# Attention probabilities transposed by DMA instead of by TensorE, and scaled after the sum over keys

## What is computed

```python
x = x + xattn(layernorm(x), ctx)   # ctx: (128, 257, 96); 16 heads of 64
x = x + wkv(layernorm(x))          # time mixing with scans over the 32 tokens
x = x + moe(layernorm(x))          # 8 experts, argmax routing

def xattn(x, ctx):                 # for every sequence b
    q, k, v = x @ Wq, ctx @ Wk, ctx @ Wv      # split in 16 heads
    attn = softmax(q @ k.T / 8)               # (16 heads, 32 tokens, 257 keys)
    return (attn @ v, heads joined) @ Wo + bo
```

## Time and profile before

| what | value |
|---|---|
| median of 3 runs | 1026.83 us |
| the profiled execution, its own time | 1028.92 us |
| span of the profiled execution | 1027.0 us, 29818 instructions |
| busy in the span: PE / DVE / ACT / POOL | 85% / 81% / 67% / 75% |
| DMA packets' time, hardware queue | 15.9% of 16 engines |
| mean granted TensorE clock | 0.935 |

### The profile page before, as it was taken

One profiled execution on the slowest core, in us unless ns is written; L12 is line 12 of the kernel. 1 busy time (PEld: TensorE's weight loads), 2 busy tenths in 40 slices (PEclk: granted clock), 3 DMA queues, 4 the chain that ended last, 5 costly groups with the idle time before them and its releaser, 6 DMA issues.

```text
span 1027.0 us, 29818 instructions
## 1 busy us (share of the span) xinstructions
PE 870.6 (85%) x8554; PEld 720.6 (70%) x8554; DVE 831.1 (81%) x2343; ACT 684.0 (67%) x2029; POOL 774.3 (75%) x1237
## 2 busy tenths in 40 slices
PE   7989998999999999999999999999998461049895
PEld 7777786878787887878787887887776261036664
DVE  5899888989999989899999999998988657025563
ACT  3777776778777778778777777777775113037774
POOL 5788888898989898888889898989886503735554
PEclk9999999999999999999999999999999655559998
DMA  9111111111111111111111211111100840111120
GB/s 233 33 33 33 32 33 33 33 33 36 49 42 32 31 31 31 31 31 31 31 31 32 59 33 31 31 31 31 31 2 2 129 162 14 52 43 53 47 54 17
DMA packets 56836, 45.11 MB, mean 44 GB/s; under 512 B 8367, under 2 KB 54578, under 8 KB 56769
## 3 DMA queue, kind: packets, MB, share of 16 engines
q1 hardware_dynamic: 54464, 40.01, 15.9%
q0 software_dynamic: 2304, 4.25, 1.3%
HBM read 37.25 MB, written 7.52 MB: 44 GB/s over the span
## 4 chain that ended last, share of the span: by engine, by line
PE 36%; POOL 31%; issue 13%; DVE 12%; ACT 4%; DMA 1%; POOLq 1%; DVEq 1%; ACTq 0%; SPq 0%
POOL Pn L925 10%; PE bank L396 6%; PE bank L373 6%; PE bank L420 4%; POOL cT L916 4%; PE bank L1369 3%; PE bank L413 3%; PE bank L385 3%; POOL sorted_rows L1232 3%; POOL chi L906 2%; PE bank L1384 2%; DVE cs L839 2%; DVE nmax L783 2%; POOL clo L910 2%; DVE Tl L777 1%
## 5 line engine op out<-in xcount | busy, mean ns | idle before, releaser
L925 POOL TENSOR_TENSOR Pn<-Pe,rsum 128x1028 f32<-128x1028 f32 x128 | 243.1, 1899 | 74.4 <-DVE rsum L798 74.4
L713 ACT ACTIVATE Pe<-bank,nmax 128x257 f32<-128x257 f32 x512 | 240.5, 475 | 30.1 <-DVE nmax L783 29.5
L783 DVE TENSOR_REDUCE nmax<-bank 128x1 f32<-128x257 f32 x512 | 202.0, 415 | 35.3 <-PE bank L373 34.0
L373 PE MATMUL bank<-cT,qh 96*128 96x257 f16 x1024 | 184.8, 275 | 21.1 <-ACT Pe L713 19.6
L777 DVE TENSOR_TENSOR Tl<-bank,Th 128x512 f16<-128x512 f32 x256 | 173.8, 680 | 0.5 <-ACT Th L702 0.4
L702 ACT ACTIVATE Th<-bank 128x512 f16<-128x512 f32 x256 | 141.3, 595 | 48.5 <-PE bank L420 48.5
L420 PE MATMUL bank<-identf,Pn 128*128 128x128 f32 x1024 | 149.3, 274 | 0.0
L373 PE MATMUL bank<-cT,ql 96*128 96x257 f16 x512 | 139.2, 272 | 0.0
L420 PEld LDWEIGHTS bank<-identf,Pn 128*128 128x128 f32 x1024 | 115.1, 142 | 6.1
L373 PEld LDWEIGHTS bank<-cT,qh 96*128 96x128 f16 x1024 | 90.3, 97 | 38.3 <-issue 15.9
L713 ACT ACTIVATION_READ_ACCUMULATOR Pe<-bank,nmax 128x1 f32 x512 | 103.8, 203 | 0.0
(11 more groups left out here) (213 smaller groups left out, 2444.4 us busy)
## 6 DMA issues: line engine op xcount, KB each, us to landing
rawT<-in_dram SPq DMA_DIRECT2D x32, 385.5 KB, 3.9
raw<-in_dram SPq DMA_DIRECT2D x32, 384.0 KB, 4.4
sorted_rows<-fill SPq DMA_DIRECT2D x1, 2620.0 KB, 21.1
xs<-sorted_rows SPq DMA_DIRECT2D x40, 65.5 KB, 1.8
R<-in_dram SPq DMA_DIRECT2D x4, 512.0 KB, 5.9
Z<-last_rows SPq DMA_DIRECT2D x128, 2.2 KB
w1r<-in_dram SPq DMA_DIRECT2D x4, 512.0 KB, 13.7
w2fr<-in_dram SPq DMA_DIRECT2D x4, 512.0 KB, 14.2
```

Of the source, the lines that this page charges most:

```text
L373: last = nc.tensor.matmul(bank[SB[t]][:, 0:M], w[:, par, b, t * P:(t + 1) * P], cT[:, s4, c, 0:M], start=(k == 0), stop=(k == 2))
L713: nc.scalar.activation(Pe[:, n_par(j + 1), t, :], bank[SB[t]][:, 0:M], ACT.Exp, bias=nmax[:, n_par(j + 1), t:t + 1], accum_out=sums[:, n_p ...
L783: nc.vector.tensor_reduce(nmax[:, n_par(j + 1), t:t + 1], bank[SB[t]][:, 0:M], AX.X, ALU.max, negate=True).then_inc(s_nmax, 1)
L925: nc.gpsimd.tensor_tensor(Pn[:, par, :, :], Pe[:, par, :, :], rsum[:, par, :].unsqueeze(2).broadcast_to([P, QT, M]), ALU.mult)\
```

## The change

Scores now lie in four neighbouring banks (`quad`), two groups for each maximum. exp is not normalised and keeps no sums. Groups 2 and 3 go to Pe in SBUF, groups 0 and 1 stay in PSUM, in place. ScalarE rounds each pair to the f16 hi half; the lo half is made by VectorE (groups 0, 1) and GpSimd (groups 2, 3). Hi and lo lie in PHL, 2560 f16 columns, and one crossbar DMA on SP transposes all of it to PT (20 blocks of 128x128). `pe_pv` has the transposed probabilities as stationary operand and 97 context columns moving, 28 matmuls; the 97th column is 1, so it gives the row sum. VectorE takes the reciprocal of that column and scales the output into On. ScalarE and GpSimd split On into Ohl, and a second crossbar DMA (8 blocks) transposes it to OT, from which `pe_y` takes every fourth column. The sum over 16 heads is now kept in PSUM over four steps and added to x once. SP runs the pipeline too. Z is loaded once. chi moves from GpSimd to ScalarE. `pe_y` and the mixing come one step later.

The core of the diff, with lines left out at "...":

```diff
+        ORDER = (2, 3, 0, 1)
...
-        def pe_scores(n, par, b, s4, tiles):
+        def pe_scores(n, par, b, s4):
...
+            for k, t in enumerate(ORDER):
+                if t >= 2:
+                    wait(nc.tensor, s_exp, QT * (n - 1) + k + 1)
+                elif t == 0:
+                    wait(nc.tensor, s_Pl, n)
...
+        def pe_pv(n, par, s8, turns):
+            wait(nc.tensor, s_PT[par], 16 * turns)
...
+            wait(nc.tensor, s_On, n)
             for t in range(QT):
+                for k, (hl, w) in enumerate(((0, chi), (0, clo), (1, chi))):
+                    for c in range(MC):
+                        nc.tensor.matmul(O5[:, t, :], PT[:, par, (2 * t + hl) * MC + c, :], w[:, s8, c, 0:CW],
+                                         start=(k == 0 and c == 0), stop=False)
+                z = Z[:, bass.ds(n, 1), 0:CW].rearrange("p o c -> p (o c)")
+                last = nc.tensor.matmul(O5[:, t, :], PT[0:R3, par, QT * 2 * MC + t, :], z, start=False, stop=True)
             last.then_inc(s_PV, 1)
...
+                    o = OT[0:CC, gp, hl * QT + h // QT, :, :].rearrange("p b r -> p (b r)")[:, h % QT:GB * P:QT]
+                    last = nc.tensor.matmul(bank[7][:, 0:C], o, w[:, h, :],
+                                            start=(h == 0 and k == 0), stop=(h == H - 1 and k == 2))
...
         def pe_step(it, j):
             n, g, jj, gp = where(it, j)
             if exists(n + 1):
...
+                pe_scores(n + 1, ((j + 1) // GB) % NP2, (j + 1) % GB, (j + 1) % 4)
+            if exists(n - 1):
+                pe_pv(n - 1, (j - 1) % NP2, (j - 1) % NC8, 4 * it + (j - 1) // 2 + 1)
             if exists(n + 5):
-                pe_mix_free(it, j)
                 pe_q(n + 5, (j + 1) % GB, bass.ds(P * (g + 1 + (jj + 1) // GB), P))
...
-            if exists(n):
-                pe_probsT(n, n_par(j), 1)
...
         def act_step(it, j):
             n, g, jj, gp = where(it, j)
+            if exists(n + 4):
...
+                act_chi(n + 4, (j + 4) % NC8, par, (j + 4) % GB)
...
+                act_cT(n + 4, (j + 4) % 4, par, (j + 4) % GB)
+            if exists(n + 1):
+                p = n_par(j + 1)
+                for k, t in enumerate(ORDER):
+                    if k == 0:
+                        wait(nc.scalar, s_Pm, n)
+                    if k % 2 == 0:
+                        wait(nc.scalar, s_nmax, 2 * (n + 1) + k // 2 + 1)
+                    dst = Pe[:, p, t - 2, :] if t >= 2 else bank[t][:, 0:MP]
+                    nc.scalar.activation(dst, bank[t][:, 0:MP], ACT.Exp, bias=nmax[:, p, t:t + 1]).then_inc(s_exp, 1)
+                    if k == 1:
+                        wait(nc.scalar, s_PT[p], 16 * (4 * it + (j + 1) // 2))
+                    if k % 2:
+                        src = Pe[:, p, :, 0:MK] if t >= 2 else quad[:, 0:2, 0:MK]
+                        wait(nc.scalar, s_exp, QT * (n + 1) + k + 1)
+                        nc.scalar.activation(Pmain[:, p, t - 1:t + 1, 0, :], src, ACT.Copy).then_inc(s_Ph, 1)
+            if exists(n + 5):
+                act_q(n + 5, (gp + 1 + (jj + 1) // GB) % NP2, (j + 1) % GB)
             if exists(n - 1):
...
+                wait(nc.scalar, s_On, n)
+                nc.scalar.activation(Ohl[:, p, 0, :, 0:CC], On[:, p, :, :], ACT.Copy).then_inc(s_Oh, 1)
+            act_mix(*mixed(it, j))
...
         def dve_step(it, j):
             n, g, jj, gp = where(it, j)
+            if exists(n + 1):
+                dve_max(n + 1, n_par(j + 1), 0)
+            dve_stat_waits(it, j, g, jj)
+            if exists(n + 1):
+                dve_max(n + 1, n_par(j + 1), 1)
             dve_stat(it, j, g, jj, gp)
+            dve_mix_a(*mixed(it, j))
...
+            if exists(n - 1):
...
+                wait(nc.vector, s_PV, n)
+                nc.vector.reciprocal(rsum[:, p, :], O5[:, :, CC]).then_inc(s_rec, 1)
+                wait(nc.vector, s_rec, n)
+                nc.vector.tensor_tensor(On[:, p, :, :], O5[:, :, 0:CC], rsum[:, p, :].unsqueeze(2).broadcast_to([P, QT, CC]),
+                                        ALU.mult).then_inc(s_On, 1)
+            if exists(n + 1):
+                p = n_par(j + 1)
+                wait(nc.vector, s_Ph, 2 * (n + 1) + 2)
+                nc.vector.tensor_copy(Plast[:, p, 0:2, 0:2], quad[:, 0:2, MK:MP]).then_inc(s_hl, 1)
+                nc.vector.tensor_tensor(Pmain[:, p, 0:2, 1, :], quad[:, 0:2, 0:MK], Pmain[:, p, 0:2, 0, :], ALU.subtract)
+                wait(nc.vector, s_hl, n + 2)
+                nc.vector.tensor_tensor(Plast[:, p, 0:2, 2:3], quad[:, 0:2, MK:M], Plast[:, p, 0:2, 0:1],
+                                        ALU.subtract).then_inc(s_Pl, 1)
+            dve_mix_b(*mixed(it, j))
             if exists(n + 5):
                 dve_q(n + 5, (gp + 1 + (jj + 1) // GB) % NP2, (j + 1) % GB)
...
         def pool_step(it, j):
+            if exists(n + 4):
+                pool_clo(n + 4, (j + 4) % NC8, ((j + 4) // GB) % NP2, (j + 4) % GB)
+                pool_cT(n + 4, (j + 4) % 4, ((j + 4) // GB) % NP2, (j + 4) % GB)
             if exists(n + 1):
...
+                wait(nc.gpsimd, s_Ph, 2 * (n + 1) + 1)
+                nc.gpsimd.tensor_tensor(Pmain[:, p, 2:4, 1, :], Pe[:, p, :, 0:MK], Pmain[:, p, 2:4, 0, :], ALU.subtract)
+                nc.gpsimd.tensor_copy(Plast[:, p, 2:4, 0:2], Pe[:, p, :, MK:MP]).then_inc(s_hm, 1)
...
+            if exists(n - 1):
+                p = n_par(j - 1)
+                wait(nc.gpsimd, s_Oh, n)
+                nc.gpsimd.tensor_tensor(Ohl[:, p, 1, :, 0:CC], On[:, p, :, :], Ohl[:, p, 0, :, 0:CC], ALU.subtract)\
+                    .then_inc(s_Ol, 1)
...
+            def sp_step(it, j):
...
+                if exists(n):
+                    p = n_par(j)
+                    wait(sp, s_PV, n - 1)
...
+                    wait(sp, s_Pl, n + 1)
+                    sp.sem_inc(s_go)
+                    wait(sp, s_Pm, n + 1)
...
+                    sp.dma_start(PT[:, p, :, :], PHL[:, p, :], transpose=True).then_inc(s_PT[p], 16)
+                if jj == 0 and exists(g + 2, G) and (n_static(n) is None or g >= 0):
+                    load_ctx(g + 2, gp)
+                if exists(n - 2):
+                    wait(sp, s_y, GB * (2 * it + (j - 2) // GB) - GB)
...
+                    wait(sp, s_Ol, n - 1)
+                    sp.sem_inc(s_go)
+                    sp.dma_start(OT[:, (j - 2) // GB % NP2, :, (j - 2) % GB, :], Ohl[:, n_par(j - 2), :, :, :], transpose=True)\
+                        .then_inc(s_OT[(j - 2) % 8], 16)
```

More of the change, by code:

```diff
@@ L178, in perceiver_layer_kernel @@
         s_bo = sem("s_bo")
-        s_raw0 = sem("s_raw0")
+        s_pad = sem("s_pad")
         s_ctx = [sem(f"s_ctx{i}") for i in range(NP2)]
+        s_ctxT = [sem(f"s_ctxT{i}") for i in range(NP2)]
         s_chi = sem("s_chi")
@@ L186, in perceiver_layer_kernel @@
         s_zd = sem("s_zd")
[L187 removed]
+        s_z = sem("s_z")
         s_cTh = sem("s_cTh")
[L189 removed]
         s_cT = sem("s_cT")
@@ L387, in pe_q @@
             last.then_inc(s_q, 1)
-        def pe_pv(n, par, s8, gp, b, pairs):
-            wait(nc.tensor, s_Ol, n)
-            k = 0
-            for w, p, s in ((chi, Th, s_Th), (clo, Th, None), (chi, Tl, s_Tl)):
-                for c in range(MC):
-                    if s is not None:
-                        wait(nc.tensor, s, MC * n + c + 1)
-                    nc.tensor.matmul(bank[6][0:CC, :], w[:, s8, c, :], p[:, par, c, :], start=(k == 0), stop=False)
-                    k += 1
-            wait(nc.tensor, s_L12, n + 1)
-            if b == 0:
-                wait(nc.tensor, s_z[gp], 16 * QT * pairs)
-            for t in range(QT):
-                last = nc.tensor.matmul(bank[6][0:CC, t * P:(t + 1) * P], Z[:, gp, b, t, :], L12[:, par, :],
-                                        start=False, stop=(t == QT - 1))
-            last.then_inc(s_PV, 1)
@@ L415, in pe_y @@
             last.then_inc(s_y, 1)
-        def pe_probsT(n, par, c):
-            wait(nc.tensor, s_Tl, MC * (n - 1) + c + 1)
-            for t in range(QT):
-                last = nc.tensor.transpose(bank[4 + c][:, t * P:(t + 1) * P], Pn[:, par, t, c * P:(c + 1) * P],
-                                           identf[:, :])
-            last.then_inc(s_T, 1)
         def n_static(n):
@@ L630, in pe_mix_free @@
                 wait(nc.tensor, s_m["ek"], it - 1)
-            if j == 6 and chunk(it, 3) is not None:
-                wait(nc.tensor, s_m["res"], it - 2)
             if j == -1 and chunk(it, 4) is not None:
@@ L1016, in pipeline @@
         def pipeline(eng, step):
-            for i in range(4):
+            for i in range(5):
                 for j in range(-1, 7):
                     step(i, j)
-            with eng.Fori(4, LIT - 1) as it:
+            with eng.Fori(5, LIT - 1) as it:
                 for j in range(-1, 7):
@@ L1128, in _ @@
             sp.wait_ge(s_ch, 2)
-            for r, part in enumerate((c256h, c256h, c256l)):
```

(2 more changed lines are left out.)

397 lines of the change are left out of this document (161 added, 236 removed).

## The result

The change makes the kernel slower: median 1199.24 us of four runs (1193.52 to 1202.48) against 1027.13 before on the same chip, a ratio of 1.1668 [1.1615, 1.1722]. The prediction was 997 us with a range to 1110: wrong in sign, and outside the range.

The account below looks back on a forecast made before the run. A loop through VectorE's and ScalarE's order was taken to bound the changed kernel at 5.72 us a step against 5.98. 128 steps save 33.3 us from 1028.9, ends add 3.4, the median lies 2.1 lower: 997 us, range 940 to 1110.

Parts of the forecast that it names:

- ql 0.59: VectorE's low half of the queries, a term of the loop between low half and next maximum: 0.59 us a step.
- The prediction's loop without mixing: Maximum, six ScalarE instructions, low half and ql in strict order, 5.72 us a step with 0.69 of mixing included.
- TensorE under 80% busy: A listed sign that the forecast is right, beside steps of 5.7 us.
- Freed TensorE time: Claim that TensorE and GpSimd time set free by the change gives nothing by itself.
- 28 matmuls at 0.056 = 1.57 us: TensorE's sum over keys, 97 columns each, 1.19 at the other bound; part of a 4.59 us TensorE step.
- exp, exp, round, exp, exp, round: ScalarE's piece of the loop, two exps and a rounding for each pair of groups: 2.88 us.
- the fast row: Transposing DMAs move 272 KB a us, like context loads: PT after 4.9 us, OT 3.5, engines 4.1 a step.
- the ends: One more pipeline step outside the repeated steps: +3.4 us, bounds 0 and 8.
- SP's issue time: Two transposing DMAs issued on SP at 0.83 us each, 1.7 us a step, hidden.
- A (crossbar): Rival, slower: the crossbar supplies less than the loop wants, 8.1 us a step, 1302 us; chance 0.20.
- B: Rival, no change: loop as long as the old step, 0.26 us more through dear scans and hand-overs, 1030 us; chance 0.18.
- C (much faster): Rival: the loop isn't closed, GpSimd bounds next at about 5.0 us a step, 905 us; chance 0.07.

Follow-up runs that it names:

- e4: The changed kernel with the query rows' f16 stores side by side and the stride moved to the PSUM read: 1097.57 us, ratio 1.0637 to before.
- e3: The kernel before with the query rows stored at every fourth f16 element, nothing else: 1108.38 us, ratio 1.077 to before.
- e5: e4 with queries made one step earlier, their splits ahead of ScalarE's exps and VectorE's reciprocal: ratio 1.0065 to before.
- e9: e5 with TensorE's query matmuls moved behind the output matmuls and the mixing, to the end of its step: 1009.99 us, ratio 0.9816 to before.
- e10: e9 with the last-key rows Z held in 128 rows, all but three of them zeros: 997.79 us, ratio 0.9657 to before.
- e7: e4 with 44 unneeded matmuls of 120 columns in TensorE's gap at each group end: ratio 1.0315 to before.
- e11: The changed kernel with only the last-key rows Z in 128 rows instead of 3: 1158.74 us, ratio 1.1245 to before.
- e8: e5 with a third, unread transposing DMA of 8 blocks a step, 36 blocks in place of 28: ratio 1.0634 to before.

## Why the prediction was wrong

**The step that failed first: "ql 0.59".** The prediction took the query splits over from the kernel before, and never looked at `q_view`, where the change swaps two letters, (h t) to (t h); the core of the diff above leaves that line out. ql costs 1.30 us, and ScalarE's part 1.31. ql is on the loop, as one step away from a group's end shows:

```profile
541.67 0.68 DVE L781 TENSOR_TENSOR PHL<-quad,PHL 128x512 f16<-128x512 f32 x1
...
542.33 0.56 DVE L823 TENSOR_TENSOR_SCAN cs<-onesn,fab 128x32 f32<-128x32 f32 x4
542.81 1.29 DVE L747 TENSOR_TENSOR ql<-bank,qh 96x512 f16<-96x512 f32 x1
543.91 1.25 DVE L754 TENSOR_REDUCE nmax<-quad 128x2 f32<-128x514 f32 x2
...
547.55 0.68 DVE L781 TENSOR_TENSOR PHL<-quad,PHL 128x512 f16<-128x512 f32 x1
```

From low half to low half are 547.55 - 541.67 = 5.88 us; less 0.48 for the scans in front of ql, 5.40. The prediction's loop without mixing is 5.72 - 0.69 = 5.03; with the true ql (1.30 in place of 0.68, so 0.62 more) and less 0.11, since the next maximum starts 1.10 behind ql where 1.21 would follow from the sum, it is 5.54. So here the loop is close to the prediction with its true ql in it. The layout is worth 102 us (e4), and 79 in the kernel before (e3).

**The dependence that the prediction had no term for: ql to scores.** The loop was closed through VectorE's and ScalarE's order alone, and TensorE was taken to be always ahead. At each fourth step the scores wait for the ql that the same loop makes last, so that round, query splits, scores and maximum come one behind the other. This left 1097.57 us in e4, where the forecast's 997 had the right ql. Making the queries a step earlier and last on TensorE takes 59 and 26 us off (e5, e9), what the clock gives back included. That e10's 997.79 us meets the forecast's 997 is chance: it is another kernel, with ql outside the stretch that the sum was made of.

**The clock.** TensorE under 80% busy was listed as a sign of being right. But its idle time comes in pieces, 3.7 us in the mean and 4.7 at most, and at each group end between 300 and 700 us a stretch at 0.50 follows, 8 us of it in the windows above. Freed TensorE time was taken to give nothing by itself; taken in such pieces it costs. At e4's layout this is 33 us (e7).

**"28 matmuls at 0.056 = 1.57 us"** is 4 x 0.52 = 2.07. The 97 columns behind a 128-column weight load are cheaper than taken (0.044 in e10, so 1.24 for 28, next to the lower bound of 1.19), but the three-row matmul costs 0.21 more four times, 0.83. TensorE's step was 5.1 us, not 4.59: with the clock at 0.85 it is 6.0. Its total is still under the 7.21 us of a step. But it did not stop counting: 0.83 us less of it a step took 41 us off the changed kernel (e11), since it lies in the chain at the group's end.

**Right:** exp 0.472 and 0.435 (taken 0.46); a maximum of 514 elements 0.681 (0.68); exp, exp, round, exp, exp, round from 522.29 to 525.13, 2.84 (2.88); On 0.557 (0.55); GpSimd's low half 1.13 (1.04) and Ol 0.91 (0.85); PT landing 4.2 and OT 2.8 us (4.9, 3.5), so the fast row was the right one to take; the ends: the first PT starts at 28.0 us (the first normalisation at 24.8), and 1200.7 - 957.6 = 243.1 us pass from the last to the end of the span (242.7 before), 3.6 in all (3.4). SP's issue time was wrong: 2.56 and 1.23 us where 0.83 each was taken, but it was hidden.

**The rivals.** A (crossbar) had the right sign and the wrong cause: TensorE waited for PT 3.8 us in all, and DMA is 0.70 busy. But its 5.0 us a step, where 4.1 was taken, is a bound close by (e8). The 1309 ns a block of the Trainium skill ("VectorE: DVE Perf Modes", section "The three transpose paths") is no rate: 20 blocks land in 4.2 us. B was nearest in kind, a loop longer than its sum. But its causes, dear scans and hand-overs, are not what the runs show, and it had 0.26 us a step where 1.34 above the old step were measured. C (much faster) did not come: the loop is closed. The range took 940 to 1110 for bounds of known terms, and had no room for a term that was missing.

## What to carry over

Price every instruction whose access pattern a diff touches, not only those it adds; here a f16 store with a stride in SBUF cost twice the time on ScalarE and VectorE, and the same permutation was free on the PSUM side. In a software pipeline walk each cross-engine wait that occurs only every few steps (here the group's end) to where its producer now stands in its engine's order. When a change takes work from TensorE, ask whether its idle time comes in one piece, since the clock that followed was here paid for by the next step. With care for all this the change can pay: the change plus four small edits (layout, queries a step ahead, queries last, no three-row matmul) is 3.4% faster than before, where the change alone is 16.7% slower.

## What the hardware showed that was not expected

- The same 96x512 split, f32 in PSUM to f16 in SBUF: ScalarE 586 and VectorE 674 ns with the f16 elements side by side, 1311 and 1302 with every fourth one written; with the stride on the PSUM read instead, 586 and 674.
- A matmul with 3 rows between matmuls of 128 rows costs TensorE 0.21 us more than one of 128 rows (0.52 against 0.31 us for seven; e10).
- A transposing DMA holds SP's queue for 2.56 us with 20 blocks and 1.23 with 8: by the two sizes 0.11 us a block and 0.34 fixed. It lands 4.2 and 2.8 us from its issue.
- Idle pieces of TensorE of 1.3 us (e5) and of 4.6 us (the change) were both followed by a granted clock of 0.50, for some 6 and 8 us. Not every piece is: between 300 and 700 us e4 has 15 waits for ql, 2.4 us in the mean, and 8 stretches at 0.50.
